# One of four weight-block sums: from a DVE operation to two accumulating transfers issued by POOL

## The chip, the cores and the metric

The kernel runs on one core of a Trainium2 chip. The metric is the device time of one execution in microseconds (us); lower is better. The engines named below are PE (TensorE, matrix multiply), DVE (VectorE), ACT (ScalarE), POOL (GpSimd) and SP (SyncE, here only a queue that issues transfers). Each runs its own instructions strictly in order, and they meet through semaphores.

## The reference

For a batch of two sequences of 512 tokens with 1024 features:

```
x = x + fake_quant(layernorm(x)) @ fake_quant(ctx)          # 512x1024 by 1024x1024, per batch
h = layernorm(x)
gate = softmax([h, ratio] @ gate_w + gate_b)                # 3 experts; ratio: mean |h| of text over vision tokens
top 2 experts, chosen by token 0 of each batch, weights per token
x = x + sum over the two of  weight * ( act_e(h @ w1[e] + b1[e]) @ w2[e] + b2[e] )
```

`act_e` is tanh, gelu or silu. So there are four (batch, chosen expert) combinations, which the kernel calls pairs 0 to 3. Each needs a 512x1024x1024 product with w1 and one with w2, in float32 accuracy.

## The kernel before, in words

**Float32 by parts.** Every float32 operand is split in a rounded part (`_hi`, made by ACT) and the rest (`_lo`, made by DVE). PE makes each product as three: hi by hi, hi by lo, lo by hi.

**Weights.** A w matrix comes as four quarters of 512x512 in the buffer `raw`, which has eight slots of 128x1024. Two slots are one `region`. ACT makes `w_hi` from a region (line 643, two operations per quarter) and DVE makes `w_lo` (line 992, two operations). The two land in one of four weight slots. SP loads a region again when its last `w_lo` is made.

**First product.** For a pair, PE runs f = 0 to 7, 24 matmuls each (line 1638). After each, ACT applies the activation twice, for `act_f` (line 731) and for `a_hi` (line 737), and DVE makes `a_lo` (line 1027) and some sums of blocks of `act_f` (lines 1033 to 1058).

**Second product.** It is done by a scheme of seven block products in place of eight, numbered 0 to 6 (lines 1594 to 1611, two halves of 12 matmuls each). Such a scheme needs sums of blocks on both sides. On the weight side there are four, and they overwrite regions of `raw` in place:

- T3 (`t3_sum`, line 1005): region(8) = region(9) - region(8)
- T2 (`t2_sum`, line 1011): region(6) = region(4) + region(8). Regions 4 and 6 are the same two slots, 0 and 1, so this is an addition in place, slots 0 and 1 += slots 2 and 3. It may start when T3 is done and when `w_lo` of quarter 4 is made, which reads the old contents.
- T4 (`t4_sum`, line 1017): region(10) = region(5) - region(6). It needs T2 and `w_lo` of quarter 5.
- T1 (`t1_sum`, line 1023): region(7) = region(9) - region(6).

Quarters 6, 10, 8 and 7 of a pair are made from T2, T4, T3 and T1. Product 2 is the first that needs quarter 6.

**Where the sums stand.** The order on each engine is written out by hand. In pair 0 DVE does T3 at the end of f = 4, T2 at the end of f = 5 and T4 at the end of f = 6. In pairs 1 to 3 it does T3 in f = 1, T2 in f = 3 right behind `w_lo` of quarter 4, and T4 in f = 4 right behind `w_lo` of quarter 5. T1 follows in all pairs between the results of products 0 and 1 (`result`, line 1089).

**What else happens in pair 1.** Batch 1 has to be normalised, and its router values and its transposed h have to be made, during pair 1. POOL makes the four normalised tiles of batch 1 (`second_h_tile`, line 469, into `b2row`): tile 0 may start when DVE has added the bias of pair 1 (line 1074), and each later one when PE has transposed the one before. PE transposes tile 0 just ahead of f = 6, tile 1 ahead of f = 7, and the others between the block products (line 1433). PE does nothing else until they are there. DVE also makes the router's dot products (`gate_dot`, line 913). Behind f = 7, ACT writes the transposed tiles to `hT_hi` (line 602) and DVE to `hT_lo` (line 876).

Of the kernel before, what the change touches and what calls it, by code (L numbers as in the profile page):

```python
# [26 lines left out]
ALU = mybir.AluOpType  # L27
# [58 lines left out]
QUARTERS = 4 + NP  # L86
# [5 lines left out]
def build(nc, x, ctx_in, s1, z1, s2, z2, gate_w, gate_b, w1, b1, w2, b2, out):  # L92
# [8 lines left out]
    with ExitStack() as st:  # L101
# [12 lines left out]
        def sem(name):  # L114
            return st.enter_context(nc.semaphore(name))
# [142 lines left out]
        w_lo_ready = sem("w_lo_ready")  # L258
# [9 lines left out]
        late_hi_ready = sem("late_hi_ready")  # L268
        late_lo_ready = sem("late_lo_ready")
        t_ready = sem("t_ready")  # L270
        g2_done = sem("g2_done")
        y2_done = sem("y2_done")
        b2_used = sem("b2_used")
# [18 lines left out]
        def region(q):  # L292

            return raw[:, 2 * REGION[q]:2 * REGION[q] + 2, :].rearrange("p c (k n) -> p (c k) n", k=2)
# [97 lines left out]
        def _(pool):  # L392
            G = nc.gpsimd
# [39 lines left out]
            def h_offset(i):  # L433

                col = slice(i, i + 1)
                G.tensor_scalar(h_shift[:, col], mvh[:, i, 0:1], h_rstd[:, col], -1.0, ALU.mult, ALU.mult
                                ).then_inc(h_rstd_ready, 1)
# [23 lines left out]
            def second_h_tile(t):  # L461

                i = TT + t
                if t == 0:
                    pool.wait_ge(b2_used, TOP_K * TT)
                else:
                    pool.wait_ge(hT_ps, i)
                pool.wait_ge(h_rstd_ready, i + 1)
                G.tensor_scalar(b2row[:], xres[:, i, :], h_rstd[:, i:i + 1], h_shift[:, i:i + 1],  # L469
                                ALU.mult, ALU.add).then_inc(h_ready["pool"], 1)  # L470
# [42 lines left out]
            for t in range(TT):  # L513
                h_power(TT + t)
                h_offset(TT + t)
            for t in range(TT):
                second_h_tile(t)

        @block.scalar
        def _(act):  # L520
# [102 lines left out]
            def w_hi_chunk(n, c):  # L623

                p, q = n // QUARTERS, n % QUARTERS
                if p > 0 and q < 4:
                    act.wait_ge(g2_done, 2 * NP * (p - 1) + 2 * (q + 4))
                elif p == 0 and q == 0:
                    act.wait_ge(abs_ready, TT)
                elif p == 0 and q in (2, 3):  # L630
                    act.wait_ge(attn_done, B * TT)
                elif q in (4, 5):
                    act.wait_ge(g1_done, p * KT + TT)
                elif q in (6, 7):
                    act.wait_ge(g1_done, p * KT + KT)
                elif q > 7:
                    act.wait_ge(g2_done, 2 * NP * p + 2 * (q - 7))
                t_sum = {8: 1, 6: 2, 10: 3, 7: 4}.get(q)
                if t_sum:
                    act.wait_ge(t_ready, 4 * p + t_sum)  # L640
                else:
                    act.wait_ge(raw_in[2 * REGION[q] + c], 16 * (2 + 2 * p + (1 if q < 4 else 2)))
                nc.scalar.activation(w_hi[n % SLOTS][:, 2 * c:2 * c + 2, :], region(q)[:, 2 * c:2 * c + 2, :],  # L643
                                     ACT.Copy).then_inc(w_hi_ready, 1)
# [73 lines left out]
            for p in range(PAIRS):  # L718
# [34 lines left out]
                q = QUARTERS * p  # L753
# [24 lines left out]
        def _(dve):  # L778
# [8 lines left out]
            V = nc.vector  # L787
# [208 lines left out]
            def w_lo_quarter(n):  # L996

                for c in range(2):
                    w_lo_chunk(n, c)
# [4 lines left out]
                    dve.wait_ge(raw_in[slot], 16 * (2 + 2 * p + 2))  # L1004
                V.tensor_tensor(region(8), region(9), region(8), ALU.subtract).then_inc(t_ready, 1)

            def t2_sum(p):

                dve.wait_ge(t_ready, 4 * p + 1)
                dve.wait_ge(w_lo_ready, 2 * (QUARTERS * p + 4) + 2)  # L1010
                V.tensor_tensor(region(6), region(4), region(8), ALU.add).then_inc(t_ready, 1)

            def t4_sum(p):

                dve.wait_ge(t_ready, 4 * p + 2)
                dve.wait_ge(w_lo_ready, 2 * (QUARTERS * p + 5) + 2)
                V.tensor_tensor(region(10), region(5), region(6), ALU.subtract).then_inc(t_ready, 1)

            def t1_sum(p):

                dve.wait_ge(t_ready, 4 * p + 3)
                dve.wait_ge(w_lo_ready, 2 * (QUARTERS * p + 6) + 2)
                V.tensor_tensor(region(7), region(9), region(6), ALU.subtract).then_inc(t_ready, 1)  # L1023

# [185 lines left out]
            for p in range(PAIRS):  # L1210
                q = QUARTERS * p
                if p == 1:
                    gate_dot(3)
                    gate_dot(4)
                for f in range(KT):
                    k = f - TT
                    dve.wait_ge(act_ready, p * KT + f + 1)
                    a_lo_block(p, f)
                    if f < TT:
                        s3_sum(p, f)  # L1220
                    else:
                        s1_sum(p, k)
                        if k:
                            s1_lo(p, k - 1)
                            s2_sum(p, k - 1)
                            s4_sum(p, k - 1)
                    if f == 0:
                        if p > 0:
                            w_lo_quarter(q + 3)
                        else:  # L1230
                            pass
                    elif f == 1:
                        if p > 0:
                            t3_sum(p)
                        else:
                            pass
                    elif f == 2 and p == 0:
                        w_lo_quarter(2)
                        w_lo_quarter(3)
                    if f < TT:  # L1240
                        bias_add(p, f)
                    if p == 0 and f == 0:
                        h_stats(5)
                        h_stats(6)
                    elif p == 0 and f == 1:
                        h_stats(7)
                        gate_dot(0)
                    elif p == 0 and f == 2:
                        gate_dot(1)
                        gate_dot(2)  # L1250
                    elif p == 1 and f in (0, 1):
                        gate_dot(5 + f)
                    elif p == 1 and f == 2:
                        gate_dot(7)
                        gate_dot(8)
                    elif p == 1 and f in (3, 4, 5):
                        gate_dot(6 + f)
                    if f == 3:
                        w_lo_quarter(q + 4)
                        if p > 0:  # L1260
                            t2_sum(p)
                    elif f == 4:
                        w_lo_quarter(q + 5)
                        if p > 0:
                            t4_sum(p)
                        else:
                            t3_sum(p)
                    elif f == 5 and p == 0:
                        t2_sum(p)
                    elif f == 6 and p == 0:  # L1270
                        t4_sum(p)
                    if p == 1 and f == TT:
                        tokens_abs(1)
                if p == 1:
                    h_lo(1, 0)
                    h_lo(1, 1)
                s1_lo(p, 3)
                s2_sum(p, 3)
                s4_sum(p, 3)
                w_lo_quarter(q + 6)  # L1280
                late_lo(p, 0)
                result(p, 0)
                if p == 1:
                    h_lo(1, 2)
                t1_sum(p)
                result(p, 1)
                if p == 1:
                    router_bias(1)
                    dot_scores()
                    score_steps()  # L1290
                w_lo_quarter(q + 7)
                late_lo(p, 1)
                if p == 1:
                    h_lo(1, 3)
                w_lo_quarter(q + 8)
                result(p, 2)
                late_lo(p, 2)
                result(p, 3)
                w_lo_quarter(q + 9)
                if p == 1:  # L1300
                    choose_experts(1)
                result(p, 4)
                late_lo(p, 3)
                w_lo_quarter(q + 10)
                result(p, 5)
                if p + 1 < PAIRS:
                    w_lo_quarter(q + QUARTERS)
                    w_lo_quarter(q + QUARTERS + 1)
                result(p, 6)
                if p == 1:  # L1310
                    gate_values(1)
                if p + 1 < PAIRS:
                    w_lo_quarter(q + QUARTERS + 2)
# [380 lines left out]
```

## Time and profile before

| | us |
|---|---|
| median of 3 runs | 404.01 (403.53 to 404.82) |
| the profiled execution | 403.35 |
| its span, first to last instruction | 401.5 |
| PE busy | 384.8 |
| DVE busy | 347.2 |
| ACT busy | 195.2 |
| POOL busy | 53.6 |

The span is covered by a profile of each instruction. "Busy" leaves out the issue of transfers and the waits on semaphores. Matmuls overlap, so a matmul that lasts 0.39 us starts 0.23 us after the one before it.

### The profile page before, as it was taken

The numbers are of one execution on the slowest core, as the hardware profiler recorded it, in microseconds if no ns is written. First come the engines' busy times: TensorE is split into PE (matmuls) and PEld (weight loads), VectorE is DVE, ScalarE is ACT, GpSimd is POOL, SyncE is SP. The second block draws the span as 40 slices with busy tenths as digits, with TensorE's granted clock in tenths as the row PEclk, the third lists the DMA queues.
The fourth block names the chain that finished last, engine by engine and source line by source line (L and its number), as shares of the span: only waits on it lengthen the run. The fifth ranks groups of instructions, "written<-read, shape, count | busy, mean of one in ns | idle before, by whom it ended". The sixth has DMA issues, their size and how long they took to land.

```text
span 401.5 us, 5230 instructions
## 1 busy us (share of the span) xinstructions
PE 384.8 (96%) x1860; PEld 303.4 (76%) x1860; DVE 347.2 (86%) x539; ACT 195.2 (49%) x253; POOL 53.6 (13%) x70
## 2 busy tenths in 40 slices
PE   1999999999999999999989999999999999999996
PEld 1435737888888888888867888888888888888885
DVE  8799869999999799999999997694997865949973
ACT  3568645174447625651846263343476333424720
POOL 8648400530000000063100000000000000000000
PEclk9999999999999999999998999999999999999999
DMA  8996049441006585000000499400055880000112
GB/s 316 411 408 282 2 137 376 169 148 61 2 0 205 177 299 211 2 0 2 0 0 2 147 379 385 189 0 2 0 176 192 241 283 2 0 0 2 53 52 106
DMA packets 23981, 54.39 MB, mean 135 GB/s; under 512 B 1776, under 2 KB 1808, under 8 KB 23824
## 3 DMA queue, kind: packets, MB, share of 16 engines
q1 hardware_dynamic: 23888, 54.01, 37.5%
q8 instruction: 15, 0.25, 0.3%
q14 instruction: 14, 0.11, 0.1%
q10 hardware_dynamic: 64, 0.02, 0.0%
HBM read 49.83 MB, written 4.19 MB: 135 GB/s over the span
## 4 chain that ended last, share of the span: by engine, by line
PE 84%; DVE 9%; ACT 2%; issue 2%; DMA 1%; ACTq 1%; POOL 0%; DVEq 0%; POOLq 0%
PE ps L1638 43%; PE ps L1607 34%; PE ps L1401 4%; DVE xres L867 2%; DVE hT_lo L876 1%; DMA b1n<-in_L_ffn_b_dram 1%; DVE bn L796 1%; DVE xres L1089 1%; PE ps L1433 1%; DVE w_lo L992 1%; PE ps L1389 1%; DVE raw L1023 1%; PE ps L1333 0%; DVE q L830 0%; DVE act_f L1058 0%
## 5 line engine op out<-in xcount | busy, mean ns | idle before, releaser
L643 ACT ACTIVATE w_hi<-raw 128x1024 fp32r<-128x1024 f32 x88 | 88.5, 1053 | 45.6 <-DVE raw L1023 22.6
L992 DVE TENSOR_TENSOR w_lo<-raw,w_hi 128x1024 fp32r<-128x1024 f32 x88 | 103.6, 1219 | 0.6
L1638 PE MATMUL ps<-hT_hi,w_hi 128*128 128x512 f32 x256 | 99.9, 390 | 0.0
L1638 PE MATMUL ps<-hT_hi,w_lo 128*128 128x512 f32 x256 | 99.6, 389 | 0.0
L1638 PE MATMUL ps<-hT_lo,w_hi 128*128 128x512 f32 x256 | 99.6, 389 | 0.0
L1607 PE MATMUL ps<-w_hi,a_hi 128*128 128x512 f32 x224 | 88.2, 394 | 2.6 <-DVE w_lo L992 2.5
L1607 PE MATMUL ps<-w_lo,a_hi 128*128 128x512 f32 x224 | 87.7, 391 | 0.0
L1607 PE MATMUL ps<-w_hi,a_lo 128*128 128x512 f32 x224 | 87.6, 391 | 0.0
L731 ACT ACTIVATE act_f<-ps,b1T 128x512 f32<-128x512 f32 x32 | 22.1, 690 | 109.1 <-PE ps L1638 109.0
L1638 PEld LDWEIGHTS ps<-hT_hi,w_hi 128*128 128x128 f32 x256 | 48.1, 188 | 10.2 <-issue 0.2
L1638 PEld LDWEIGHTS ps<-hT_hi,w_lo 128*128 128x128 f32 x256 | 48.1, 188 | 10.0
L1638 PEld LDWEIGHTS ps<-hT_lo,w_hi 128*128 128x128 f32 x256 | 48.1, 188 | 9.8
L1607 PEld LDWEIGHTS ps<-w_hi,a_hi 128*128 128x128 f32 x224 | 42.4, 189 | 12.1 <-issue 3.2
L1089 DVE SCALAR_TENSOR_TENSOR xres<-ps,gate,xres 128x512 f32<-128x512 f32 x56 | 40.1, 744 | 11.7 <-PE ps L1607 11.7
L1607 PEld LDWEIGHTS ps<-w_lo,a_hi 128*128 128x128 f32 x224 | 42.5, 190 | 8.8
L1607 PEld LDWEIGHTS ps<-w_hi,a_lo 128*128 128x128 f32 x224 | 42.4, 189 | 8.9
L1027 DVE TENSOR_TENSOR a_lo<-act_f,a_hi 128x256 fp32r<-128x256 f32 x32 | 13.4, 419 | 24.8 <-ACT a_hi L737 24.7
L1401 PE MATMUL ps<-ctxq,q1T 128*128 128x512 f16 x128 | 31.4, 386 | 1.7 <-DVE xres L867 1.1
L469 POOL TENSOR_SCALAR b2row<-xres,h_rstd,h_shift 128x1024 f32<-128x1024 f32 x4 | 11.6, 2900 | 102.2 <-DVE xres L1074 86.6
L1401 PEld LDWEIGHTS ps<-ctxq,q1T 128*128 128x128 f16 x128 | 11.4, 98 | 17.4 <-issue 5.4
L671 ACT ACTIVATE a_hi<-act_f 128x1024 fp32r<-128x1024 f32 x16 | 16.9, 1058 | 12.1 <-PE ps L1607 12.1
L1074 DVE SCALAR_TENSOR_TENSOR xres<-b2row,gate,xres 128x1024 f32<-128x1024 f32 x16 | 20.5, 1279 | 0.0
(156 smaller groups left out, 369.7 us busy)
## 6 DMA issues: line engine op xcount, KB each, us to landing
raw<-in_L_ffn_w_dram SPq DMA_DIRECT2D x64, 512.0 KB, 5.6
raw<-in_ctx_dram SPq DMA_DIRECT2D x16, 512.0 KB, 11.5
xres<-in_x_dram SPq DMA_DIRECT2D x8, 512.0 KB, 9.5
out_dram<-xres SPq DMA_DIRECT2D x16, 256.0 KB, 4.2
b2row<-in_L_ffn_b_dram SPq DMA_DIRECT2D x4, 512.0 KB, 6.8
gate_rows<-in_L_ffn_gate_w_dram SPq DMA_DIRECT2D x1, 1536.0 KB, 18.3
small<-in_L_xattn_x_scale_dram ACTq DMA_DIRECT2D x2, 0.0 KB
small<-in_L_xattn_x_zp_dram ACTq DMA_DIRECT2D x2, 0.0 KB
```

Of the source, the lines that this page charges most:

```text
L469: G.tensor_scalar(b2row[:], xres[:, i, :], h_rstd[:, i:i + 1], h_shift[:, i:i + 1], ALU.mult, ALU.add).then_inc(h_ready["pool"], 1)
L643: nc.scalar.activation(w_hi[n % SLOTS][:, 2 * c:2 * c + 2, :], region(q)[:, 2 * c:2 * c + 2, :], ACT.Copy).then_inc(w_hi_ready, 1)
L671: nc.scalar.activation(dst[:], src, ACT.Copy).then_inc(late_hi_ready, 1)
L731: nc.scalar.activation(act_f[:, f, :], ps[:, G1_BANK + f % 2, :], EXPERT_ACT[ee], bias=bias)
L867: last = V.scalar_tensor_tensor(out=xt, in0=ps[:, ATT_BANK[b][t] + c, :], scalar=s12, in1=xt, op0=ALU.mult, op1=ALU.add)
L992: V.tensor_tensor(w_lo[n % SLOTS][:, 2 * c:2 * c + 2, :], region(n % QUARTERS)[:, 2 * c:2 * c + 2, :], w_hi[n % SLOTS][:, 2 * c:2 * c + 2, ...
L1027: V.tensor_tensor(a_lo[f // TT][:, f % TT, :], act_f[:, f, 0:2 * P], a_hi[f // TT][:, f % TT, :].bitcast(F32), ALU.subtract).then_inc(a_lo ...
L1074: V.scalar_tensor_tensor(out=xt, in0=b2row[:], scalar=gate[:, p * TT + t:p * TT + t + 1], in1=xt, op0=ALU.mult, op1=ALU.add).then_inc(b2_u ...
L1089: V.scalar_tensor_tensor(out=xt, in0=ps[:, bank + j, :], scalar=gate[:, p * TT + t:p * TT + t + 1], in1=xt, op0=ALU.mult, op1=ALU.add).the ...
L1401: T.matmul(ps[:, ATT_BANK[b][t] + c, :], q1T[b][:, k, t * P:(t + 1) * P], ctxq[b][:, k, c * H:(c + 1) * H], start=k == 0, stop=False)
L1607: last = T.matmul(ps[:, bank + j, :], a[slot][:, k, tok], v[w][:, k, :], start=fresh and n == 0, stop=n == 3 * TT - 1, skip_group_check=True)
L1638: last = T.matmul(ps[:, G1_BANK + f % 2, :], w[q % SLOTS][:, k % TT, fs], h[:, k, :], start=n == 0, stop=n == 3 * KT - 1)
```

## The change

T2 leaves DVE. POOL issues two transfers from slots 2 and 3 to slots 0 and 1 of `raw`, which add to what is there (`accum_op`), each 128x1024 float32 or 512 KB, and both count up a new semaphore, `t2_in`, by 16. T4 on DVE and the making of `w_hi` of quarter 6 on ACT wait for both (`t2_in` at 32 per pair). The semaphore `t_ready` now counts three sums for each pair, and not four. POOL's T2 of pairs 0 and 1 stands ahead of the four tiles of `second_h_tile`, that of pairs 2 and 3 behind them.

```diff
@@ gpsimd
+            def t2_sum(p):
+
+                pool.wait_ge(t_ready, 3 * p + 1)
+                pool.wait_ge(w_lo_ready, 2 * (QUARTERS * p + 4) + 2)
+                for c in range(2):
+                    G.dma_start(region(6)[:, 2 * c:2 * c + 2, :], region(8)[:, 2 * c:2 * c + 2, :],
+                                accum_op=ALU.add).then_inc(t2_in, 16)
+
+            t2_sum(0)
+            t2_sum(1)
             for t in range(TT):
                 second_h_tile(t)
+            t2_sum(2)
+            t2_sum(3)
@@ scalar, w_hi_chunk
-                t_sum = {8: 1, 6: 2, 10: 3, 7: 4}.get(q)
-                if t_sum:
-                    act.wait_ge(t_ready, 4 * p + t_sum)
+                t_sum = {8: 1, 10: 2, 7: 3}.get(q)
+                if q == 6:
+                    act.wait_ge(t2_in, 32 * p + 32)
+                elif t_sum:
+                    act.wait_ge(t_ready, 3 * p + t_sum)
@@ vector
-            def t2_sum(p):
-
-                dve.wait_ge(t_ready, 4 * p + 1)
-                dve.wait_ge(w_lo_ready, 2 * (QUARTERS * p + 4) + 2)
-                V.tensor_tensor(region(6), region(4), region(8), ALU.add).then_inc(t_ready, 1)
-
             def t4_sum(p):
 
-                dve.wait_ge(t_ready, 4 * p + 2)
+                dve.wait_ge(t2_in, 32 * p + 32)
...
             def t1_sum(p):
 
-                dve.wait_ge(t_ready, 4 * p + 3)
+                dve.wait_ge(t_ready, 3 * p + 2)
...
                     if f == 3:
                         w_lo_quarter(q + 4)
-                        if p > 0:
-                            t2_sum(p)
...
-                    elif f == 5 and p == 0:
-                        t2_sum(p)
```

POOL's last instructions, before. The L469 rows are the four tiles of `second_h_tile` (`b2row`); brackets hold the semaphores that a row waits for.

```order
66 L436 TENSOR_SCALAR h_shift<-mvh,h_rstd 128x1 [waits pool_step]
67 L469 TENSOR_SCALAR b2row<-xres,h_rstd,h_shift 128x1024 [waits h_rstd_ready,b2_used]
68 L469 TENSOR_SCALAR b2row<-xres,h_rstd,h_shift 128x1024 [waits h_rstd_ready,hT_ps] x3
69 L101 UNCONDITIONAL_BRANCH
```

The same place after the change.

```order
66 L437 TENSOR_SCALAR h_shift<-mvh,h_rstd 128x1 [waits pool_step]
67 L522 DMA raw<-raw 128x1024 [waits w_lo_ready,t_ready]
68 L522 DMA raw<-raw 128x1024
69 L522 DMA raw<-raw 128x1024 [waits w_lo_ready,t_ready]
70 L522 DMA raw<-raw 128x1024
71 L470 TENSOR_SCALAR b2row<-xres,h_rstd,h_shift 128x1024 [waits h_rstd_ready,b2_used]
72 L470 TENSOR_SCALAR b2row<-xres,h_rstd,h_shift 128x1024 [waits h_rstd_ready,hT_ps] x3
73 L522 DMA raw<-raw 128x1024 [waits w_lo_ready,t_ready]
74 L522 DMA raw<-raw 128x1024
75 L522 DMA raw<-raw 128x1024 [waits w_lo_ready,t_ready]
76 L522 DMA raw<-raw 128x1024
```

Four issues (pairs 0 and 1) stand ahead of tile 0, with two new waits, and four behind tile 3.

DVE in pair 1, f = 3 and f = 4, before: `w_lo` of quarter 4, T2 (L1011), the f = 4 block, `w_lo` of quarter 5, T4 (L1017).

```order
237 L992 TENSOR_TENSOR w_lo_56<-raw,w_hi_55 128x1024 [waits w_hi_ready] x2
238 L1011 TENSOR_TENSOR raw<-raw 128x2048 [waits w_lo_ready,t_ready]
239 L1027 TENSOR_TENSOR a_lo_65<-act_f,a_hi_64 128x256 [waits act_ready]
240 L1039 TENSOR_TENSOR act_f<-act_f 128x256 [waits s3_ready]
241 L913 SCALAR_TENSOR_TENSOR ps,dot<-xres,mvh,gate_rows 128x1024 [waits dots_done,rows_in,h_stats_ready]
242 L992 TENSOR_TENSOR w_lo_50<-raw,w_hi_49 128x1024 [waits w_hi_ready] x2
243 L1017 TENSOR_TENSOR raw<-raw 128x2048 [waits w_lo_ready,t_ready]
```

The same place after the change.

```order
236 L1007 TENSOR_TENSOR w_lo_56<-raw,w_hi_55 128x1024 [waits w_hi_ready] x2
237 L1036 TENSOR_TENSOR a_lo_65<-act_f,a_hi_64 128x256 [waits act_ready]
238 L1048 TENSOR_TENSOR act_f<-act_f 128x256 [waits s3_ready]
239 L928 SCALAR_TENSOR_TENSOR ps,dot<-xres,mvh,gate_rows 128x1024 [waits dots_done,rows_in,h_stats_ready]
240 L1007 TENSOR_TENSOR w_lo_50<-raw,w_hi_49 128x1024 [waits w_hi_ready] x2
241 L1026 TENSOR_TENSOR raw<-raw 128x2048 [waits w_lo_ready,t2_in]
```

T2 is gone from DVE, and T4 (now L1026) waits for the transfers. PE and SP keep their order.

## Rows read from the trace of the kernel before

**Rows 1.** The page: busy time of each engine

```profile
PE 384.8 (96%) x1860; PEld 303.4 (76%) x1860; DVE 347.2 (86%) x539; ACT 195.2 (49%) x253; POOL 53.6 (13%) x70
```

**Rows 2.** Chain of waits, 90 to 260 us: start, us, what

```profile
106.83 38.08 PE ps L1607 x168
...
177.55 0.87 PE ps L1433 x8
...
190.87 0.47 ACT a_hi L737
...
193.59 2.48 DVE hT_lo L876 x4
...
210.22 1.15 DVE w_lo L992
...
211.50 23.53 PE ps L1607 x96
```

**Rows 3.** Waits of PE: engine line waited for: total, times, longest

```profile
PE ps L1607 <- DVE w_lo L992: 2.5, 1, 2.5
```

**Rows 4.** Timeline of DVE in pair 1: start, us, instruction

```profile
172.00 2.36 DVE L992 TENSOR_TENSOR w_lo<-raw,w_hi 128x1024 fp32r<-128x1024 f32 x2
174.47 2.95 DVE L1011 TENSOR_TENSOR raw<-raw 128x2048 f32<-128x2048 f32 x1
...
178.01 1.60 DVE L913 SCALAR_TENSOR_TENSOR ps<-xres,mvh,gate_rows 128x1024 f32<-128x1024 f32 x1
...
179.54 2.35 DVE L992 TENSOR_TENSOR w_lo<-raw,w_hi 128x1024 fp32r<-128x1024 f32 x2
181.99 2.95 DVE L1017 TENSOR_TENSOR raw<-raw 128x2048 f32<-128x2048 f32 x1
...
191.37 0.42 DVE L1027 TENSOR_TENSOR a_lo<-act_f,a_hi 128x256 fp32r<-128x256 f32 x1
```

**Rows 5.** Timeline of POOL, tiles of batch 1; last: idle before

```profile
170.69 4.59 POOL L469 TENSOR_SCALAR b2row<-xres,h_rstd,h_shift 128x1024 f32<-128x1024 f32 x1 [86.58 <-DVE xres L1074]
178.53 4.27 POOL L469 TENSOR_SCALAR b2row<-xres,h_rstd,h_shift 128x1024 f32<-128x1024 f32 x1 [3.25 <-PE ps L1433]
...
196.67 1.26 POOL L469 TENSOR_SCALAR b2row<-xres,h_rstd,h_shift 128x1024 f32<-128x1024 f32 x1 [10.33 <-PE ps L1433]
```

**Rows 6.** Timeline of PE at f = 6 of pair 1

```profile
177.39 1.03 PE L1433 MATMUL ps<-ident,b2row 128*128 128x128 f32 x8
```

**Rows 7.** Timeline of DVE in pair 0

```profile
97.96 2.29 DVE L1005 TENSOR_TENSOR raw<-raw 128x2048 f32<-128x2048 f32 x1
...
106.21 2.29 DVE L1017 TENSOR_TENSOR raw<-raw 128x2048 f32<-128x2048 f32 x1
...
115.00 1.40 DVE L1089 SCALAR_TENSOR_TENSOR xres<-ps,gate,xres 128x512 f32<-128x512 f32 x2
```

**Rows 8.** Timeline of PE in pair 0, first matmul of product 2

```profile
117.55 0.39 PE L1607 MATMUL ps<-w_hi,a_hi 128*128 128x512 f32 x1
```

**Rows 9.** Timeline of DVE in pair 2

```profile
262.37 2.29 DVE L1011 TENSOR_TENSOR raw<-raw 128x2048 f32<-128x2048 f32 x1
...
267.71 2.29 DVE L1017 TENSOR_TENSOR raw<-raw 128x2048 f32<-128x2048 f32 x1
...
274.24 0.42 DVE L1027 TENSOR_TENSOR a_lo<-act_f,a_hi 128x256 fp32r<-128x256 f32 x1 [2.30 <-ACT a_hi L737]
...
279.68 0.43 DVE L1027 TENSOR_TENSOR a_lo<-act_f,a_hi 128x256 fp32r<-128x256 f32 x1 [3.43 <-ACT a_hi L737]
```

**Rows 10.** The loads of `raw`: issue on SP (ns min/median/max), landing

```profile
L325 SPq DMA_DIRECT2D raw<-in_L_ffn_w_dram x64: 372/373/628, 54.8 to 327.0; - x64
...
DMA to landing us min/median/max: 3.8/6.4/15.4
```

**Rows 11.** Stretches with and without transfers

```profile
core 0: us, PE busy (x) PEld busy (x) DVE busy (x) ACT busy (x) POOL busy (x), PEclk, DMA share, GB/s
...
174.30:186.00 11.70, 11.70 (x62) 9.84 (x61) 11.49 (x13) 4.42 (x8) 6.39 (x3) 1.00 0.00 0
225.00:240.00 15.00, 15.00 (x68) 12.43 (x67) 14.52 (x27) 7.29 (x7) 0.00 (x0) 1.00 0.93 328
```

More of the change, by code:

```diff
@@ L270, in build @@
         t_ready = sem("t_ready")
+        t2_in = sem("t2_in")
         g2_done = sem("g2_done")
```

## The prediction, made before the changed kernel ran

> **What bounds the kernel now.** I read the busy times first, then PE's waits, then the chain of waits, and last the timelines of DVE, POOL and PE about each T2. PE is busy for 384.8 of the 401.5 us, and DVE for 347.2 [rows 1]. So a faster DVE is worth something only where PE waits for it, and past the start PE has one such wait of note: 2.5 us on `w_lo` [rows 3]. The chain says where: PE resumes at 211.50, behind a `w_lo` of pair 1 [rows 2]. All of pair 0's second product is one unbroken run of PE, 38.08 us for 168 matmuls [rows 2], or 2.72 us for each half product.
>
> Next I followed that one wait back. From 211.50 the chain goes back through DVE to `hT_lo` at 193.59, from there to ACT's `a_hi` of f = 7, which ends at 190.87 + 0.47 = 191.34, and from there to PE, with the transposes ahead of f = 6 in it at 177.55 [rows 2]. T2 of pair 1 (174.47) and T4 (181.99) are not on it. DVE's `a_lo` of f = 7 starts at 191.37 [rows 4], just behind that `a_hi`: whatever backlog DVE had in f = 3 to 6 was worked off there.
>
> **What the change removes.** Four operations, one per pair: 2.29 us as in pair 2 [rows 9], and 2.95 in pair 1 [rows 4], 9.8 us of DVE in all. None pays. Pair 0 and pairs 2 and 3 have no wait of PE for DVE. In pair 1 DVE would only come earlier to `a_lo` of f = 7, which waits for PE and ACT. Worth 0, at most the 2.5 us.
>
> **What it adds: POOL's place in the queue.** T2 of pair 1 waits for `w_lo` of quarter 4, made at 172.00 + 2.36 = 174.36 [rows 4]. Tile 0 now stands behind it. Before, tile 0 ran from 170.69 to 175.28 [rows 5], and PE took it at 177.39 with nothing else to do [rows 6]. Now POOL first issues two transfers from 174.4. No row shows an issue by POOL. SP takes 0.37 us for one [rows 10], the short end; the long end I take as POOL's longest tile, 4.59. My estimate is 1.1 each, nearer SP's, with some more since POOL writes its own descriptors, so tile 0 starts at 176.6. How long it takes depends on DVE: 1.26 us for tile 3, but 4.59 and 4.27 for tiles 0 and 1 [rows 5], which ran under an unbroken train of DVE operations with two SBUF inputs. Tile 0 ended 0.8 us after DVE's short pause at 174.36 to 174.47, tile 1 0.8 us after that at 181.89 to 181.99 [rows 4, 5], and both times the DVE operation started then took 2.95 in place of 2.29. So POOL gets in only when DVE pauses. In the new order `w_lo` of quarter 5 moves ahead by T2's 2.9 us, from 179.54 to about 176.7 until 179.0 [rows 4], and then T4 waits and DVE pauses. Tile 0 then ends at 179.0 + 1.3 = 180.3, for any issue up to 2.3 us each, and PE is late by 180.4 - 177.4 = **3.0 us**. Without the exclusion it would be 176.6 + 1.3 = 177.9, or 0.5.
>
> The Trainium skill has this as a rule (SBUF — State Buffer, on the port that VectorE and GpSimd share): a DVE instruction with two SBUF inputs shuts out a GpSimd instruction that reads SBUF for its whole length. By that rule, the trace agrees: the term is 3.0 and not 0.5.
>
> Is it recovered at the 2.5 us wait? No. The chain behind f = 7 (ACT, `hT_lo`, the sums, T1, `w_lo`) is released by PE, so it moves by the same 3.0.
>
> **What it adds: the latency of T2.** Let L be the time from the last of T3 and `w_lo` of quarter 4 to the landing of both transfers. The new waiter on DVE is T4, and all of DVE stands behind it: the blocks of f = 5 to 7, `w_lo` of quarter 6 and the results. Parts of L: first issue 1.1; a fixed part; the moving. A load of the same 512 KB lands at best in 3.8 us [rows 10]. The bus moves 328 GB/s at a share of 0.93, so 353 when full [rows 11]; 0.524 MB is then 1.5 us, and the fixed part 2.3. An accumulating transfer must read the addend and the destination, 2.1 MB for both, at that rate 5.9 us. L = 1.1 + 2.3 + 5.9 = **9.3**. The queues are empty meanwhile (share 0.00 [rows 11]). The short end, by the written bytes alone: 1.1 + 2.3 + 3.0 = 6.4. The long end is the longest landing of a load, 15.4 [rows 10]. I take 9.3, as both streams surely have to be read.
>
> The Trainium skill has another price (DMA: Bandwidth & Descriptors, Anatomy of one DMA): about 2.0 us plus the bytes over 436 GB/s, for a transfer issued from GpSimd. An estimate by that page would be L near 5.5, the sum then 3.0 us and the time 407.0; it says nothing of accumulating ones, and no run here shows it yet.
>
> What L costs, pair by pair:
> - Pair 0: T3 ends at 100.2, T4 ended before at 106.21 + 2.2 = 108.4 [rows 7]. Now it ends at 100.2 + L + 2.3, later by L - 5.9. DVE has no idle time from there to the first result, which ended at 115.00 + 0.70 = 115.7; product 2, which overwrites that bank, begins at 117.55 [rows 7, 8]. Slack 1.8. Cost L - 7.7, or 9.3 - 7.7 = **1.6**. Removing T2 gives nothing here.
> - Pair 1: T4 ended at 184.9, 6.5 us ahead of `a_lo` of f = 7, which may now be 3.0 later [rows 4]. So T4 may end at 187.9, and L may be 187.9 - 2.3 - 174.4 = 11.2. Cost 0.
> - Pairs 2 and 3: `w_lo` of quarter 4 is done at 262.3. T4 ended at 270.0, and DVE was idle for 2.30 + 3.43 us behind it [rows 9], so T4 may end at 275.7, and L may be 275.7 - 2.3 - 262.3 = 11.1. Then follows a slack like pair 0's. Cost 0.
>
> **Sum.** 3.0 + 1.6 = 4.6 us on the profiled execution's 403.35 (span 401.5 and 1.85 around it), 407.95. The median of the runs stands 0.66 above the profiled one, so the forecast is 404.01 + 4.6 = **408.6**.
>
> **Rivals.**
> - *The transfers are slow.* The adding may be slower than reading both streams. For: no row shows one, and loads took up to 15.4 us, though in a crowd. At L = 15.4: pair 0 7.7, pair 1 3.0 + 4.2, pairs 2 and 3 each 4.3 - 1.8 = 2.5, together 19.9, or 423.9; at L = 13, 5.3 + 4.8 + 0.2 = 10.3, or 414.3. PE's waits would then be longest in pair 0.
> - *The transfers are fast (L under 7.7), and only POOL's order costs.* 3.0, or 407.0.
> - *Nothing is felt.* Both issues are over by 175.5 and tile 0 gets in at DVE's small gaps, and L is under 7.7. 404.0. For: 1.26 us fits before 177.39. Against: `gate_dot` of 1.60 [rows 4] stands just there, and tiles 0 and 1 were shut out under it before.
> - *Faster.* The 2.95 us that pair 1 saves on DVE reach the wait at 211.50 and take it away: 2.5 us, 401.5. It decides if DVE's own backlog, and not `a_hi`, sets 191.37, and if tile 0 is in time. Against: `a_hi` ends at 191.34, and `hT_lo` behind it is released by ACT [rows 2].
>
> **How the numbers follow.** Forecast 0.52 (L 7.7 to 12, tile 0 late by 2 to 4 us: 405.9 to 413). Slow transfers 0.22, fast ones with POOL's order 0.12, nothing felt 0.10, faster 0.04. A measurement of this kernel can tell about 0.3%, 1.2 us, from no change. So slower 0.52 + 0.22 + 0.12 = 0.86, same 0.10, faster 0.04. The range leaves out the last two cases, and the slow transfers' upper part (L over about 13.8): 405.4 to 418.
>
> **What would show it.** In the changed kernel's profile: a wait of PE for POOL at the transposes ahead of f = 6 of pair 1, of about 3.0 us (right for the first term); tile 0 ending about 1.3 us after DVE's last `w_lo` of quarter 5; T4 waiting for a transfer in every pair, by L less about 5 us; a wait of PE at product 2 of pair 0 of about 1.6 us; none in pairs 2 and 3; and the wait of 2.5 us at product 3 of pair 1 still there. I am wrong if PE does not wait ahead of f = 6, if the transfers land in under 7.7 or over 12 us, or if the 2.5 us are gone.

## The result, and the profile after

| | before | after |
|---|---|---|
| median of 3 runs, us | 404.01 (403.53 to 404.82) | 408.05 (407.54 to 408.21) |
| ratio to before, with its 95% interval | 1 | 1.0094 (1.0065 to 1.0124) |
| profiled execution, span | 403.35, 401.5 | 407.54, 405.7 |
| DVE busy, POOL busy | 347.2, 53.6 | 336.4, 57.2 |

Slower by 4.0 us at the median. Repeated unedited on another chip, the changed kernel had 408.58 beside 404.64 before, which is 1.0097 by these medians; the ratio on record, from all executions, is 1.0128 (1.0088 to 1.0169). Two executions, 1694.39 us in run 1 and 491.72 of the kernel before beside runs 1 to 4, are far out of line with all others and are left out of every number here.

DVE is busy for 10.8 us less, and PE shows new waits. PE's waits in the profile after, in the form "who waited <- for whom: us in total, times, longest":

```profile
PE ps L1612 <- DVE w_lo L1007: 2.5, 1, 2.5
PE ps L1438 <- POOL b2row L470: 2.2, 1, 2.2
...
PE ps L1612 <- issue: 0.6, 1, 0.6
```

The first is the wait of [rows 3], unchanged. The second and third are new. They are these two rows of PE's timeline (start, us, instruction; in brackets the idle time before):

```profile
119.20 0.47 PE L1612 MATMUL ps<-w_hi,a_hi 128*128 128x512 f32 x1 [0.57 <-issue]
...
181.54 1.09 PE L1438 MATMUL ps<-ident,b2row 128*128 128x128 f32 x8 [2.21 <-POOL b2row L470]
```

The first is the start of product 2 of pair 0 [rows 8], the second the transposes of tile 0 ahead of f = 6 of pair 1 [rows 6]. For the first the profile names no releaser ("issue"); that it is the late T4 of pair 0, runs 2, 9 and 10 show. POOL's timeline about the latter answers to [rows 5]:

```profile
176.60 1.74 POOL L522 DMA_DIRECT2D raw<-raw  x2 [73.12 <-DVE w_lo L1007]
177.73 3.76 POOL L470 TENSOR_SCALAR b2row<-xres,h_rstd,h_shift 128x1024 f32<-128x1024 f32 x1
182.75 1.20 POOL L470 TENSOR_SCALAR b2row<-xres,h_rstd,h_shift 128x1024 f32<-128x1024 f32 x1 [1.26 <-PE ps L1438]
```

POOL issues the two transfers, and only then makes tile 0, until 181.49; PE takes it at 181.54. DVE's timeline in the same place answers to [rows 4]:

```profile
173.71 2.35 DVE L1007 TENSOR_TENSOR w_lo<-raw,w_hi 128x1024 fp32r<-128x1024 f32 x2
...
176.66 1.60 DVE L928 SCALAR_TENSOR_TENSOR ps<-xres,mvh,gate_rows 128x1024 f32<-128x1024 f32 x1
...
178.17 2.36 DVE L1007 TENSOR_TENSOR w_lo<-raw,w_hi 128x1024 fp32r<-128x1024 f32 x2
183.75 2.33 DVE L1026 TENSOR_TENSOR raw<-raw 128x2048 f32<-128x2048 f32 x1 [3.22 <-DMA raw<-raw]
...
195.57 0.43 DVE L1036 TENSOR_TENSOR a_lo<-act_f,a_hi 128x256 fp32r<-128x256 f32 x1 [3.08 <-ACT a_hi L752]
```

T4 (L1026) waits 3.22 us for the transfers, and `a_lo` of f = 7 then waits 3.08 us for ACT: what DVE was spared turned into idle time of DVE. In pair 0, where T3 ends at 98.89 + 2.28 = 101.17 and T4 starts at 109.56, the wait does reach PE:

```profile
98.89 2.28 DVE L1020 TENSOR_TENSOR raw<-raw 128x2048 f32<-128x2048 f32 x1
...
109.56 2.29 DVE L1026 TENSOR_TENSOR raw<-raw 128x2048 f32<-128x2048 f32 x1 [4.10 <-DMA raw<-raw]
```

**Where the 4.2 us between the two spans lie.** I measured from PE's first matmul of the first w1 product, which lies behind everything that was not changed:

```profile
63.01 0.50 PE L1638 MATMUL ps<-hT_hi,w_hi 128*128 128x512 f32 x1
```

```profile
63.95 0.50 PE L1643 MATMUL ps<-hT_hi,w_hi 128*128 128x512 f32 x1
```

(Before first, then after.) From there to the end it is 401.5 - 63.01 = 338.5 us before and 405.7 - 63.95 = 341.8 after. So 3.3 us belong to the change, 0.7 at product 2 of pair 0 and 2.4 at tile 0 among them, and 0.9 lie in the first 63 us, which it does not touch. The experiments are read by this second number, from the first w1 product to the end, which I call the rest.

### The profile page after: what moved, and what is told of

The parts are those of the page before. It is cut to its first block, busy times and chain, and to the rows that moved or that the text cites. A ratio compares the mean times of both kernels' runs of the same rounds, so it can differ in the third digit from the quotient of the medians.

```text
span 405.7 us, 5234 instructions
## 1 busy us (share of the span) xinstructions
PE 385.4 (95%) x1860; PEld 303.2 (75%) x1860; DVE 336.4 (83%) x535; ACT 195.0 (48%) x253; POOL 57.2 (14%) x78
## 4 chain that ended last, share of the span: by engine, by line
PE 73%; DVE 17%; issue 3%; DMA 3%; ACT 2%; POOL 2%; SPq 1%; DVEq 0%; POOLq 0%; ACTq 0%
PE ps L1643 35%; PE ps L1612 33%; DVE w_lo L1007 3%; PE ps L1406 3%; DVE ps L928 3%; DMA raw<-in_ctx_dram 3%; DVE xres L882 2%; DVE hT_lo L891 1%; DVE bn L811 1%; DVE xres L1083 1%; DVE xres L1098 1%; POOL b2row L470 1%; PE ps L1438 1%; DVE raw L1020 1%; PE ps L1394 1%
## 5 line engine op out<-in xcount | busy, mean ns | idle before, releaser
L522 POOL DMA_DIRECT2D raw<-raw x8 | 7.3, 1063 | 234.2 <-DVE w_lo L1007 217.8
L1026 DVE TENSOR_TENSOR raw<-raw 128x2048 f32<-128x2048 f32 x4 | 9.2, 2303 | 13.9 <-DMA raw<-raw 13.9
```

## The experiments

Times are medians. The first four stood beside 404.42 for the kernel before, the next four beside 404.64, the last two, with one run each, beside 403.67. "Rest" is from the profile of each: 338.5 before, 341.8 after.

**1. Tile 0 ahead of POOL's T2 of pair 1.**

```diff
             t2_sum(0)
+            second_h_tile(0)
             t2_sum(1)
-            for t in range(TT):
+            for t in range(1, TT):
                 second_h_tile(t)
```

> The changed kernel, with POOL's T2 of pair 1 put behind tile 0 of batch 1 and ahead of tile 1; nothing else moves. My theory (2.4 us of the loss are tile 0 standing behind the two issues): tile 0 ends at about 175 to 177 as before the change, PE does not wait ahead of f = 6, T4 of pair 1 lands about 1 us later without harm, and the time falls by 2.4 us, from 408.05 to about 405.6. Rival (the loss is the latency of the transfers, DVE held at T4, and POOL's order only coincides): PE's wait moves elsewhere and the time stays at 408.0, within 0.5.

Measured: 405.53, ratio to before 1.0032 (1.0009 to 1.0055); rest 339.5, which is 2.3 less than the changed kernel's. PE has no wait for POOL. POOL's timeline:

```profile
172.96 4.58 POOL L470 TENSOR_SCALAR b2row<-xres,h_rstd,h_shift 128x1024 f32<-128x1024 f32 x1 [68.99 <-DVE xres L1084]
177.48 1.78 POOL L522 DMA_DIRECT2D raw<-raw  x2
180.83 2.18 POOL L470 TENSOR_SCALAR b2row<-xres,h_rstd,h_shift 128x1024 f32<-128x1024 f32 x1 [1.57 <-PE ps L1439]
```

This is the largest part of the loss, and it is the place in POOL's queue, not the transfers: they are issued here as well, even later, and cost nothing in pair 1.

**2. T4 of pair 0 behind the block of f = 7.**

```diff
-                    elif f == 6 and p == 0:
+                    elif f == 7 and p == 0:
                         t4_sum(p)
```

> The changed kernel, with T4 of pair 0 moved from the end of f = 6 to the end of f = 7, so that DVE does the block of f = 7 while the transfers run. My theory: DVE's idle 4.1 us at T4 shrink by about 0.7 (the block of f = 7 may start at 108.8, T4 then at 110.7), PE's wait of 0.57 us at product 2 of pair 0 goes, and the time falls by 0.6 to 407.5. Rival (that PE wait comes from something else than the late T4): no change, 408.05. A null by less than 0.3 would leave it open.

Measured: 406.96, ratio to before 1.0067 (1.0046 to 1.0087). The pause of PE ahead of product 2, beyond the usual spacing, fell from 0.72 to 0.26 us, by 0.46 where 0.6 was expected. It is not quite gone because in this profile a transfer landed later (8.4 us from issue at the longest, 7.3 in the changed kernel), and T4 starts only at 111.18; in run 6, with the same move and 7.3 again, the pause is 0.04. The rest is 340.9; of its 0.8 gain about 0.3 are not from here: in this profile the clock did not fall behind the 2.5 us wait (below). So the late T4 of pair 0 is the second part.

**3. T2 by transfer in pairs 2 and 3 alone.**

```diff
+            for t in range(TT):
+                second_h_tile(t)
+            t2_transfer(2)
+            t2_transfer(3)
...
-                        if p > 0:
+                        if p == 1:
                             t2_sum(p)
```

(Here `t2_transfer` is the changed kernel's `t2_sum` on POOL; the counts of `t_ready` are adapted.)

> The kernel before, with T2 as two accumulating transfers in pairs 2 and 3 alone; pairs 0 and 1 keep T2 on DVE, and POOL issues behind all its tiles. My theory (there the latency is covered by DVE's idle time, and a faster DVE gains nothing): DVE waits 3.3 us at T4 in pairs 2 and 3, PE waits nowhere new, 404.0, within 0.5. Rival 1 (a transfer issued by POOL costs the program something at its start, which would be the 0.9 us by which the changed kernel was already late at the first products): 404.9, with the same 0.9 in the first 20 us of the profile. Rival 2 (DVE's wait reaches PE also there): 406 or more.

Measured: 403.93, ratio 0.9989 (0.9976 to 1.0003); rest 338.7. DVE waits for the transfers twice, and PE has no new wait:

```profile
DVE raw L1037 <- DMA raw<-raw: 6.9, 2, 3.6
```

So 6.9 us of waits and 4.6 us of saved operations both vanish: DVE's idle time covers the one and swallows the other. The first w1 product started at 63.80 here, and this kernel has transfers by POOL, so rival 1 was not yet excluded; run 7 did that.

**4. The gate_dot of f = 4 behind `w_lo` of quarter 5.**

```diff
-                    elif p == 1 and f in (3, 4, 5):
+                    elif p == 1 and f in (3, 5):
                         gate_dot(6 + f)
...
                     elif f == 4:
                         w_lo_quarter(q + 5)
+                        if p == 1:
+                            gate_dot(6 + f)
```

> The changed kernel, with the one gate_dot of f = 4 in pair 1 moved behind w_lo of quarter 5 (it then stands ahead of T4, where DVE is idle). My theory (POOL's tile gets at SBUF only when DVE's train of two-input operations pauses): the train now ends with gate_dot and is as long as before, but w_lo of quarter 5 gives way 1.6 us sooner; if any of these operations shuts POOL out, tile 0 still ends about 1 us behind the train, at the same time, and the time stays at 408.0; if only the w_lo operations do, tile 0 ends 1.6 us sooner and the time is about 406.5. Rival (the tile takes 3.8 us from its start whatever DVE does): 408.0 with the tile still 3.8 us long in either order.

Measured: 408.16 (405.65 to 409.45), too scattered to tell by time. The profile tells, and it is the branch in which the `w_lo` operations alone shut POOL out: PE's wait for tile 0 is 0.9 us in place of 2.2, the rest 339.9 (here too the clock did not fall), and tile 0 takes 2.31 us in place of 3.76. POOL, then DVE:

```profile
179.21 2.31 POOL L470 TENSOR_SCALAR b2row<-xres,h_rstd,h_shift 128x1024 f32<-128x1024 f32 x1
```

```profile
178.13 2.35 DVE L1007 TENSOR_TENSOR w_lo<-raw,w_hi 128x1024 fp32r<-128x1024 f32 x2
180.40 2.55 DVE L928 SCALAR_TENSOR_TENSOR ps<-xres,mvh,gate_rows 128x1024 f32<-128x1024 f32 x1
```

The tile ends at 181.52, 1.04 us behind the two `w_lo`, and this time the gate_dot takes 2.55 in place of 1.60, from which I take it that POOL came in ahead of it. The rival (3.8 us whatever DVE does) falls. So does a part of my own wording: POOL need not wait until DVE's train pauses. It waited for the pair of `w_lo` operations, and got in where that pair ended. Why it gets in there and not between the gate_dot and the pair behind it stays open.

**5. The changed kernel once more.**

> The changed kernel once more, unedited, so that it stands on one chip beside the next three. Theory (3.3 of the 4.2 us between the two profiled executions are the change, the other 0.9 lie in the first 20 us, ahead of anything that was changed, and differ from one execution to the next): from the first matmul of the first w1 product to the end 341.7 us in its profile again, within 0.2, whatever the start does; the time 407.3 to 408.3. Rival (the late start belongs to the changed kernel): the first w1 product starts at 64.0 or later again, and the profile of the kernel with T2 by transfer in pairs 2 and 3 (63.9) was the same effect.

Measured: 408.58 (406.95 to 412.82), above the expected times; rest 341.85, as expected. The first w1 product started at 63.85. PE's waits are the same three (2.5, 2.3 and 0.6).

**6. Both moves (of runs 1 and 2).**

> The changed kernel with both moves, tile 0 ahead of POOL's T2 of pair 1, and T4 of pair 0 behind the block of f = 7. My theory (the two waits of PE are the whole cost, and 9.8 us less on DVE gain nothing): no wait of PE for POOL nor at product 2 of pair 0, the wait of 2.5 us at product 3 of pair 1 still there, from the first w1 product to the end 338.4 to 338.8 us (338.4 before the change), and the time within 0.5 of the kernel before. Rival (DVE's relief is worth something once the two waits are gone): at least 1 us faster than before.

Measured: 404.60 beside 404.64, ratio 1.0013 (0.9996 to 1.0031); rest 338.8, the upper end of what was expected. PE waits for neither POOL nor, beyond 0.04 us, at product 2. What is left is as before:

```profile
PE ps L1613 <- DVE w_lo L1008: 2.5, 1, 2.5
```

Both waits together are the cost of the change. With them gone, some 10 us less on DVE still gain nothing. Both profiles have the fall of the clock behind the 2.5 us wait, so the comparison is a fair one.

**7. The kernel before, with DVE's order in the second half of each pair changed.**

```diff
-                if p == 1:
-                    router_bias(1)
-                    dot_scores()
-                    score_steps()
                 w_lo_quarter(q + 7)
                 late_lo(p, 1)
-                if p == 1:
-                    h_lo(1, 3)
                 w_lo_quarter(q + 8)
                 result(p, 2)
                 late_lo(p, 2)
-                result(p, 3)
-                w_lo_quarter(q + 9)
                 if p == 1:
+                    w_lo_quarter(q + 9)
+                    result(p, 3)
+                    router_bias(1)
+                    dot_scores()
+                    score_steps()
                     choose_experts(1)
+                else:
+                    result(p, 3)
+                    w_lo_quarter(q + 9)
                 result(p, 4)
                 late_lo(p, 3)
                 w_lo_quarter(q + 10)
+                if p == 1:
+                    h_lo(1, 3)
```

> The kernel before, T2 on DVE, with DVE's order behind result 1 of pair 1 changed: w_lo of quarter 7, late_lo 1, w_lo of quarter 8, result 2, late_lo 2, w_lo of quarter 9, result 3, then the router's small operations, the choice of experts, result 4, late_lo 3, w_lo of quarter 10 and last hT_lo of the last tile. In the other pairs w_lo of quarter 8 and late_lo 2 stand only where they stood. Theory (the 2.5 us wait of PE is set by what DVE does between 191.37 and 211.3, so only work taken out of there helps): the wait goes, and the 0.6 us wait one product later too, 2.5 to 3.1 us less, about 401.3. Rival (another wait takes its place, w_lo of quarter 7 itself, result 3 or late_lo 3): 402.5 or more.

Measured: 403.67 beside 404.64, ratio 0.9979 (0.9962 to 0.9997), by a small margin the fastest of all here; rest 337.15. The rival was right: the wait at product 3 shrank from 2.5 us to nothing, and one of 2.35 us came up at product 6, for `w_lo` of quarter 10:

```profile
228.99 0.47 PE L1609 MATMUL ps<-w_hi,a_hi 128*128 128x512 f32 x1 [2.35 <-DVE w_lo L992]
```

The expected 401.3 was missed. So the 2.5 us do not go with one better order, as I had expected: from 194.63 to this wait DVE pauses only twice, for 0.28 us each, so it has too much to do between f = 7 of pair 1 and quarter 10. That an order only chooses where PE feels it is my reading of this one order. Of the 1.35 us by which the rest is shorter than before, a part is the clock, which did not fall here. This kernel has no transfer by POOL, and its first w1 product started at 64.05, later than the changed kernel's 63.95. So the late start is not a property of the change.

**8. The changed kernel with both moves and that order.**

> The changed kernel with both moves (tile 0 first, T4 of pair 0 late) and DVE's new order behind result 1 of pair 1. Theory (T2 by transfer neither gains nor loses once it stands right): the same time as the kernel before with the new order alone, about 401.3, within 0.5. Rival (with the wait at product 3 gone DVE is the bound in pair 1, and T2's 2.95 us count): at least 1 us faster than that kernel.

Measured: 404.72, ratio 1.0005 (0.9991 to 1.0018). That is 1.0 us behind run 7 by the medians; the profile explains more than that. Its wait at product 6 is the same, 2.32 us, so T2's relief did not reach it, and the rival falls. The rest is 339.1, 1.9 us more than run 7's, and 1.5 of it lies in the 24 matmuls behind that wait (7.17 us in place of 5.72). Stretches of both kernels, run 8 and then run 7, with PE's granted clock in the third column from the end:

```profile
229.30:236.50 7.20, 7.17 (x25) 5.82 (x26) 7.20 (x9) 4.24 (x4) 0.00 (x0) 0.78 1.01 352
```

```profile
229.00:232.00 3.00, 3.00 (x13) 2.49 (x14) 3.00 (x5) 1.90 (x2) 0.00 (x0) 1.00 1.02 388
```

Behind equal waits, one execution was granted a lower clock and the other not. The times of all executions say the same: of run 7's twelve, six have a mean granted clock of 1.000 (median 403.04) and six of 0.996 (404.26), and of run 8's three (404.20) and nine (404.74). At an equal mean clock run 8's are still 0.5 to 1.2 us longer, the larger figure from three executions that scatter by 2.5. Whether its kernel as such is slower than run 7's is not settled.

**9. Plain transfers in place of accumulating ones** (T2 is not computed, and what is made from it is not the reference's).

```diff
-                    G.dma_start(region(6)[:, 2 * c:2 * c + 2, :], region(8)[:, 2 * c:2 * c + 2, :],
-                                accum_op=ALU.add).then_inc(t2_in, 16)
+                    G.dma_start(region(6)[:, 2 * c:2 * c + 2, :], region(8)[:, 2 * c:2 * c + 2, :],
+).then_inc(t2_in, 16)
```

> The changed kernel with plain transfers from slots 2 and 3 to slots 0 and 1 in place of the accumulating ones, so the block T2 is not computed and everything made from it is wrong. Only the latency L of T2 in pair 0 is asked for (end of T3 to start of T4; 8.4 us with the accumulating ones, of which 4.9 us with all transfer engines busy). My theory of the prediction (the destination has to be read too, so twice the bytes): half the reading, about 3.0 us of busy engines, L about 6.5. Rival (moving within SBUF has one price, adding or not): L 8.4 again, within 0.3.

Measured: L in pair 0 is 4.9 us, from the end of T3 at 100.81 to T4 at 105.67, and not the expected 6.5. The landing of the eight transfers, here and then in the changed kernel, in us from the issue (min/median/max):

```profile
DMA to landing us min/median/max: 2.9/3.4/3.8
```

```profile
DMA to landing us min/median/max: 4.5/5.7/7.3
```

The same stretch of 11 us (101 to 112) in both, with the busy share of the transfer engines as last but one column, plain and then accumulating:

```profile
101.00:112.00 11.00, 11.00 (x51) 9.09 (x50) 9.23 (x20) 5.90 (x10) 1.30 (x2) 1.00 0.25 98
```

```profile
101.00:112.00 11.00, 11.00 (x50) 9.10 (x49) 6.42 (x13) 4.00 (x7) 1.99 (x2) 1.00 0.52 98
```

11 us at 0.25 are 2.8 us of full use, at 0.52 5.7 us. Adding costs twice the moving, as a destination that is read too would; the rival (one price) falls. Whether the second half goes into that reading or into the adding itself, no run separates. A POOL issue is dearer too: in pair 0 the two take 1.99 us of POOL when they add and 1.30 when they copy. PE's wait for tile 0 is 2.2 us here as well, although the issues are shorter: the tile's end is not set by them. And with L at 4.9, below the 7.7 of the prediction, PE has no pause at product 2 of pair 0:

```profile
117.88 0.39 PE L1611 MATMUL ps<-w_hi,a_lo 128*128 128x512 f32 x1
118.11 0.39 PE L1611 MATMUL ps<-w_hi,a_hi 128*128 128x512 f32 x1
```

**10. One transfer of 1 MB.**

```diff
-                for c in range(2):
-                    G.dma_start(region(6)[:, 2 * c:2 * c + 2, :], region(8)[:, 2 * c:2 * c + 2, :],
-                                accum_op=ALU.add).then_inc(t2_in, 16)
+                G.dma_start(region(6), region(8), accum_op=ALU.add).then_inc(t2_in, 16)
```

> The changed kernel with one accumulating transfer of 1 MB for each T2 in place of two of 512 KB. Theory (the second issue, 1.1 us, is hidden behind the first one's data, and the moving sets L): L in pair 0 stays 8.4 within 0.5, and tile 0 of batch 1 starts 1 us sooner but still ends about 1 us behind w_lo of quarter 5, so PE's wait ahead of f = 6 stays about 2.3 us. Rival (each issue adds to L and to tile 0's delay): L 7.4, the wait 1.2 us.

Measured: L is 109.11 - 100.97 = 8.1 us, about 0.25 less than with two, and PE's pause at product 2 is 0.47 in place of 0.72, shorter by the same amount. PE's wait for tile 0 is 2.2 us:

```profile
176.81 4.22 POOL L470 TENSOR_SCALAR b2row<-xres,h_rstd,h_shift 128x1024 f32<-128x1024 f32 x1
```

POOL is free sooner, but the tile takes 4.22 in place of 3.76 us. The moving sets L, DVE sets the tile.

## Why the prediction was right, point by point

- **Which waits decide.** Right. DVE's relief was worth nothing (runs 3 and 6), and the loss is the two new waits of PE at the two places named; with both taken away the kernel is level with the one before.
- **Tile 0.** Right in mechanism, 3.0 us forecast, 2.4 measured. Two terms were off. The pair of `w_lo` ends 0.2 us sooner than I had (180.53, less the 1.7 by which everything is later there, is 178.8 against 179.0). And the tile needs 0.96 us behind it, where I took the whole 1.26 of an undisturbed tile; 0.9 was readable from tiles 0 and 1 before the change (175.28 - 174.36 and 182.80 - 181.89; the prediction's 0.8 counts from where DVE's next operation starts). That only a pause of DVE lets POOL in was too strong (run 4).
- **Latency.** L was forecast at 9.3 us and is 8.4 in pair 0, from 101.17 to 109.56. The issue took 1.1 us as estimated, the moving 5.7 in place of 5.9. What was too long is the fixed part. I had taken it from a loaded queue's best landing, 3.8 us, and a plain transfer of POOL's lands in 2.9.
- **Pair 0.** "L - 7.7" gives 0.7 for 8.4; measured 0.72. For 8.1 (run 10) it gives 0.4, measured 0.47, and for 4.9 (run 9) nothing, and there is none. The slack was right, the 1.6 was only L's error passed on.
- **Pairs 1 to 3.** L is 7.7 there, under the bounds of about 11 that I worked out; no cost, as run 3 shows for pairs 2 and 3 and run 1 for pair 1.
- **The sum.** 4.6 forecast, 4.0 at the medians. But the two terms measure 2.4 + 0.7 = 3.1, and the profile gives the change 3.3 in all, so that the forecast of 408.6 came within 0.6 of the median is in part luck: terms 1.5 too large met some 0.9 from elsewhere. In the profiled pair 0.9 lie in the start, which scatters (63.01 to 65.33 in the profiles of this case). A further part may be the clock behind the new wait at tile 0: it stayed high in both profiles of the changed kernel but fell in those of runs 9 and 10, and their rests are 342.0 and 342.7, although their pauses at product 2 are shorter by 0.7 and 0.25; by these sums the fall there cost 1.0 to 1.2 us more than the one behind the 2.5 us wait. How often it falls at that place in other executions no run shows: their mean granted clock is on record (0.996 in seven of the nine of the changed kernel, and in 32 of 54 of the kernel before), but not where it fell.
- **The 2.5 us wait.** That it stays was right. That it stands on operations behind f = 7 was right too, but run 7 shows that it is the amount of them and not a chain that this new order opens.

## What to carry to other kernels

Before moving an operation to another engine, look at what is queued behind it there: here an instruction that nobody waited for on DVE came to stand, with its own wait, ahead of a tile on which PE depended, and swapping two lines gave back more than half of the loss. And ask whether the engine that is relieved is waited for at all. An engine busy for 86% gave nothing back when 3% of its work was taken away, because the one place where it was late lay elsewhere.

A transfer that adds is slow for the reader (8 us for 1 MB here against 2.3 on DVE), and it is not free for the issuing engine: POOL spent 1.7 to 2.0 us on the two issues, nearly what DVE saved. It fits where the consumer is that far away, and not directly ahead of an in-order engine's next due work.

## What was not expected of the hardware

**The clock behind a wait.** The profiles of this case have 17 waits of PE of 2.2 to 2.5 us behind the start. Behind nine of them its granted clock fell from 2.4 to 1.2 GHz and stayed there for about 3 us. Stretches of the kernel before, on both sides of its wait at 211.50 (the granted clock is the third column from the end):

```profile
208.50:211.50 3.00, 0.48 (x5) 0.27 (x4) 2.83 (x14) 3.00 (x5) 0.00 (x0) 0.96 0.00 0
211.50:214.50 3.00, 3.00 (x7) 2.42 (x8) 3.00 (x4) 3.00 (x4) 0.00 (x0) 0.50 0.00 0
214.50:217.50 3.00, 3.00 (x14) 2.40 (x14) 3.00 (x4) 0.66 (x2) 0.00 (x0) 0.97 0.00 0
```

Seven matmuls start in the first 3 us behind the wait and 14 in the next. It costs up to 1.5 us (run 8; 1.2 between the medians of run 7's executions at the two mean clocks), and less where PE would have had to wait again anyway: 0.3 by run 2, where PE, at the full clock, waited another 0.63 us one product later. It did not fall behind equal waits in runs 2, 4 and 7, and in runs 9 and 10 it fell behind the 2.2 us for tile 0 and not behind the 2.5. The forecast had priced each wait of PE by its length alone.

**POOL's tile under DVE.** The same operation of 128x1024 took between 1.20 and 4.59 us. Where it ran beside `w_lo`, it ended 0.9 to 1.04 us behind the end of that pair, and the DVE operation that started then was about 0.7 to 0.95 us longer (2.95 in place of 2.29, 2.55 in place of 1.60), if it followed at once.
